# Experts' biases moved from the expert loop to the attention's projection, with gates in two parts

## What is computed

```python
xn = _layernorm(x, axis=-1)
x = x + _L0_attn_ref(xn, Wq, Wk, Wv, Wo) + _L0_ffn_ref(xn, Wg, bg, W1, b1, W2, b2)
# _L0_attn_ref: causal linear attention, Y @ Wo.T
# _L0_ffn_ref:
gate_probs = softmax(x @ Wg + bg)
_, top_idx = top_k(gate_probs, 2)
selected = gate_probs * expert_mask
selected = selected / (selected.sum(-1, keepdims=True) + 1e-08)
h = gelu(einsum('bsf,efh->bseh', x, W1) + b1)
expert_out = einsum('bseh,ehf->bsef', h, W2) + b2[None, None]
return einsum('bsef,bse->bsf', expert_out, selected)
# second layer: attention ends in  out = y @ w_proj + b_proj
```

## Time and profile before

| what | value |
|---|---|
| median of 3 runs | 354.57 us (354.26 to 354.77) |
| profiled execution | 354.33 us, its span 352.5 us |
| busy: PE, DVE, ACT, POOL | 339.4, 320.9, 271.4, 208.8 us |
| granted TensorE clock, mean | 0.995 |
| head and routing, to the first up product | 0 to 62.4 us |
| loop over slots | 62.4 to about 273 us |
| second layer | to 352.5 us |

### The profile page before, as it was taken

The page is one execution under the profiler, slowest core; times in us unless marked ns, Lnnn a source line. Parts: engine busy times, 40 slices in busy tenths (PEclk is TensorE's granted clock), DMA queues, the critical chain, the costliest instruction groups (busy, mean ns, idle before and its releaser), DMA issues.

```text
span 352.5 us, 9136 instructions
## 1 busy us (share of the span) xinstructions
PE 339.4 (96%) x2488; PEld 296.4 (84%) x2488; DVE 320.9 (91%) x633; ACT 271.4 (77%) x764; POOL 208.8 (59%) x229
## 2 busy tenths in 40 slices
PE   8999878999999999999999999999999899999995
PEld 3888334799999999999999899999998688778875
DVE  5999999899999999998899899998978799998665
ACT  2997946968887878787787678778985987777751
POOL 3899202843323666766776678778877278884110
PEclk9999989999999999999999999999999999999999
DMA  5896196454444555555555654565452002221112
GB/s 161 238 278 181 32 387 240 114 147 131 136 130 137 156 152 149 159 150 156 155 157 154 168 155 133 164 186 145 120 141 75 9 7 54 60 63 30 30 32 60
DMA packets 45520, 46.98 MB, mean 133 GB/s; under 512 B 6928, under 2 KB 33712, under 8 KB 45216
## 3 DMA queue, kind: packets, MB, share of 16 engines
q1 hardware_dynamic: 40432, 37.17, 35.7%
q0 software_dynamic: 4320, 8.86, 10.1%
q10 hardware_dynamic: 720, 0.38, 0.5%
HBM read 32.88 MB, written 13.50 MB: 132 GB/s over the span
## 4 chain that ended last, share of the span: by engine, by line
PE 86%; DVE 9%; DMA 2%; issue 2%; POOL 0%; ACT 0%; DVEq 0%; POOLq 0%
PE banks L574 18%; PE banks L561 18%; PE banks L700 7%; PE banks L701 7%; PE banks L364 4%; PE banks L1012 3%; PE banks L545 3%; PE banks L1041 2%; PE banks L1088 2%; PE banks L352 2%; PE banks L1070 2%; PE banks L1050 2%; PE banks L776 2%; PE banks L1022 2%; PE banks L1058 2%; PE banks L320 2%
## 5 line engine op out<-in xcount | busy, mean ns | idle before, releaser
L489 POOL DMA_INDIRECT xg<-xn_rows,slot_tok x71 | 76.5, 1077 | 77.0 <-PE banks L545 43.6
L591 ACT ACTIVATE xT<-banks,b1T 128x128 f32<-128x128 f32 x284 | 81.5, 375 | 18.8 <-PE banks L561 18.6
L506 POOL DMA_INDIRECT qk_exp<-expert_rows,ranki x64 | 74.0, 1156 | 19.1 <-issue 18.7
L574 PE MATMUL banks<-w_sb,xT 128*128 x568 | 78.9, 282 | 0.0
L561 PE MATMUL banks<-xgT,w 128*128 128x128 f32 x568 | 75.4, 276 | 0.0
L574 PEld LDWEIGHTS banks<-w_sb,xT 128*128 128x128 f32 x568 | 69.3, 192 | 0.5
L561 PEld LDWEIGHTS banks<-xgT,w 128*128 128x128 f32 x568 | 69.0, 192 | 0.8 <-issue 0.5
L712 DVE TENSOR_TENSOR cq<-banks,phi 128x360 f32<-128x360 f32 (+1 forms) x96 | 47.4, 548 | 7.6 <-PE banks L701 6.7
L684 DVE TENSOR_TENSOR low<-outer,high 128x1152 fp32r<-128x1152 f32 x32 | 43.5, 1358 | 3.2 <-ACT high L678 3.2
L721 DVE TENSOR_REDUCE sums<-cq 128x144 f32<-128x1152 f32 x32 | 43.0, 1343 | 0.1
L678 ACT CAST high<-outer 128x1152 fp32r<-128x1152 f32 x32 | 36.9, 1154 | 7.0 <-DVE outer L667 5.7
(11 more groups left out here) (210 smaller groups left out, 691.0 us busy)
## 6 DMA issues: line engine op xcount, KB each, us to landing
w<-in_L_ffn_W SPq DMA_DIRECT2D x71, 256.0 KB
expert_rows<-ye SPq DMA_DIRECT2D x71, 64.0 KB
expert_rows<-x_sb SPq DMA_DIRECT2D x2, 2048.0 KB, 9.7
x_sb<-in_L_attn_x SPq DMA_DIRECT2D x8, 256.0 KB, 4.0
xn_rows<-xn SPq DMA_DIRECT2D x8, 256.0 KB, 2.9
w_sb<-in_L_ffn_W SPq DMA_DIRECT2D x8, 256.0 KB, 3.9
out<-outer SPq DMA_DIRECT2D x7, 256.0 KB, 2.4
xg<-xn_rows,slot_tok POOLq DMA_INDIRECT x71
```

The source lines that it names most:

```text
L489: pool.indirect_dma_start(out=xg[n][:, :], out_offset=None, in_=xn_dram, in_offset=bass.IndirectOffsetOnAxis(ap=slot_tok[:, j:j + 1], axis ...
L506: pool.indirect_dma_start(out=y_moe[:, i, k, :], out_offset=None, in_=y_dram, in_offset=bass.IndirectOffsetOnAxis(ap=ranki[:, 0, k, i:i + ...
L574: last = nc.tensor.matmul(y, hidT[p][:, c, :], w2_sb[:, ds(e * NC + c, 1), :], start=False, stop=(c == NC - 1))
L591: last = nc.scalar.activation(hidT[p][:, c, :], slot_bank(j)[:, c * P:(c + 1) * P], ACT.Gelu_apprx_tanh, bias=b1T[:, ds(e * NC + c, 1)])
```

## The change

The bias matmul of each slot (L572) goes. b2 stands twice in a new tile `bias`: for the first tile of a batch in columns 0 to 127, for the second in columns 128 to 255, repeated on rows so that rows come in a high and a low part of b2 (`low_row`), each against a high and a low part of the gates. SP fills `bias_raw` by 16 DMAs of b2 (8 rows x 128) and two of b_proj (one row); they stand in its queue ahead of `save(0)`. ACT rounds the rows with low_row 1 (`bias_high`), POOL subtracts (`bias_parts`). DVE forms the gates of all experts (zero where not chosen) with three more operations, splits them in two parts (`split_gates`, two operations) between the first two `low`. PE transposes the split gates of two batches at a time, ACT copies them to `gT`, and one matmul per batch over 64 rows and 256 columns adds gates times bias at the projection. b_proj takes `ones_r` and `bias` in float32r in place of bf16.

```diff
+    bias_high_of = high[2][:, 0:NBIAS]
+    bias_raw = phi_all[:, 4 * D:4 * D + NBIAS]
+    gate_row = xn_all[:, 2:4, :, :].rearrange("p n c f -> p (n c f)")
+    gate_of_all = yT0[:, 0:NT * NE].rearrange("p (a e) -> p a e", e=NE)
...
-    def split_biases(pool):
...
+    def bias_high(act):
+        act.wait_ge(bias_loaded, 16 * 18)
+        nc.scalar.activation(bias_high_of, bias_raw, ACT.Copy, scale=const("low_row")).then_inc(bias_ready, 1)
+
+    def bias_parts(pool):
+        pool.wait_ge(bias_ready, 1)
+        nc.gpsimd.tensor_tensor(bias[:, :], bias_raw, bias_high_of.bitcast(f32), ALU.subtract).then_inc(bias_ready, 1)
...
-            pe.wait_ge(bias_rows, 16 * 6)
         y = slot_bank(j)[:, 0:D]
-        nc.tensor.matmul(y, ones_bf[:, :], bias3[:, ds(e * D, D)], start=True, stop=False)
...
+        if b == 0:
+            pe.wait_ge(gates_split, 1)
+        if b % 2 == 0:
+            nc.tensor.transpose(ps[6][:, 3 * P:4 * P], gate_row[:, b * NGR:(b + 2) * NGR], ident)
...
+        if b % 2 == 0:
+            nc.scalar.copy(gT[:, :], ps[6][:, 3 * P:4 * P])
...
+        rows = slice(b % 2 * NGR, (b % 2 + 1) * NGR)
+        nc.tensor.matmul(ps[5][:, 0:2 * D], gT[rows, :], bias[rows, 0:2 * D], start=False, stop=True,
+                         skip_group_check=True).then_inc(o_ps, 1)
...
-        nc.tensor.matmul(ps[4], ones_bf[:, :], bias3[:, BIASP:BIASP + D].unsqueeze(1).broadcast_to([P, GT, D]),
+        nc.tensor.matmul(ps[4], ones_r[:, :], bias[:, BIASP:NBIAS].unsqueeze(1).broadcast_to([P, GT, D]),
...
-            sp.dma_start(bias_sp[:, 0:BIASP // P], b2.rearrange("e h -> (e h)").rearrange("(p c) -> p c", p=P)).then_inc(bias_in, 16)
-            sp.dma_start(bias_sp[:, BIASP // P:NBIAS // P], b_proj.rearrange("(p c) -> p c", p=P)).then_inc(bias_in, 16)
...
+            sp.wait_ge(zeros_ready, 2)
+            for q in range(P // (2 * NE)):
+                for t in range(2):
+                    lo = (2 * q + t) * NE
+                    sp.dma_start(bias_raw[lo:lo + NE, t * D:(t + 1) * D], b2).then_inc(bias_loaded, 16)
+            for lo in (0, 32):
+                sp.dma_start(bias_raw[lo:lo + 1, BIASP:NBIAS], b_proj.rearrange("(a c) -> a c", a=1)
+                             ).then_inc(bias_loaded, 16)
...
-            sp.wait_ge(bias_split, 5)
-            sp.wait_ge(bias_zero, 1)
-            for n in range(3):
-                for lo, hi in ((0, BIASP), (BIASP, NBIAS)):
-                    sp.dma_start(bias3[n:n + 1, lo:hi].rearrange("a (p c) -> a p c", p=P),
-                                 bias_part[:, n, lo // P:hi // P]).then_inc(bias_rows, 16)
...
+            bias_high(act)
...
+                act.wait_ge(bias_ready, 2)
...
-            nc.vector.memset(bias3[:, :], 0.0).then_inc(bias_zero, 1)
+            nc.vector.memset(bias_raw, 0.0).then_inc(zeros_ready, 1)
...
+            both = TT(oh[:, 0, :, :], oh[:, 0, :, :], oh[:, 1, :, :], ALU.add)
...
-            done(RED(row(5), masked, AX.X, ALU.add))
+            RED(row(5), masked, AX.X, ALU.add)
+            v.wait_ge(route, n_route[0])
+            done(TT(gate_of_all, masked, oh[:, 0, :, :], ALU.mult))
...
+                done(TT(gate_of_all, gate_of_all, sel[0][:, :].unsqueeze(2).broadcast_to([P, NT, NE]), ALU.mult))
+
+            def split_gates():
+                whole = yT0[:, 0:NT * NE].rearrange("p (b f) -> p b f", b=B).unsqueeze(2).broadcast_to([P, B, 2, 2 * NE])
+                done(nc.vector.tensor_copy(gate_parts[:, :, :, 0, :], whole))
+                TT(gate_parts[:, :, :, 1, :], whole, gate_parts[:, :, :, 0, :].bitcast(f32), ALU.subtract
+                   ).then_inc(gates_split, 1)
...
             gates()
-            for r in range(2):
-                attn_low(v, 0, r, 0)
+            attn_low(v, 0, 0, 0)
+            split_gates()
+            attn_low(v, 0, 1, 0)
```

More of the change, by code:

```diff
@@ L22 @@
 BIG = 3.0e38
-BIASP, NBIAS = NE * D, NE * D + D
+BIASP, NBIAS = 2 * D, 3 * D
+NGR = 4 * 2 * NE
 CONSTS = {}
@@ L58, in constant_table @@
     put("row_no", row)
+    put("low_row", row // 32 % 2)
     put("rows_in_front", P * row)
@@ L99, in build @@
     NB = 4
-    xn = [sbuf(f"xn{p}", [P, GT, D]) for p in range(NB)]
+    xn_all = sbuf("xn_all", [P, NB, GT, D])
+    xn = [xn_all[:, p, :, :] for p in range(NB)]
     xT = [sbuf(f"xT{p}", [P, GT, P]) for p in range(2)]
@@ L118, in build @@
     bg_sb = sbuf("bg_sb", [P, NE])
[L119 to L122, removed]
+    bias = sbuf("bias", [P, NBIAS], f32r)
     ones_bf = sbuf("ones_bf", [P, P], bf16)
@@ L230, in build @@
     wT_ps, wT_ready = sem("wT_ps"), sem("wT_ready")
-    bias_in, bias_split, bias_rows = sem("bias_in"), sem("bias_split"), sem("bias_rows")
-    small_ready, pool_const, warmed, bias_zero = sem("small_ready"), sem("pool_const"), sem("warmed"), sem("bias_zero")
+    bias_in, bias_loaded, bias_ready = sem("bias_in"), sem("bias_loaded"), sem("bias_ready")
+    small_ready, pool_const, warmed, gates_split = sem("small_ready"), sem("pool_const"), sem("warmed"), sem("gates_split")
     zeros_ready = sem("zeros_ready")
@@ L569, in down @@
             pe.wait_ge(w2_in, 16 * NE)
-            pe.wait_ge(bias_rows, 16 * 6)
         y = slot_bank(j)[:, 0:D]
-        nc.tensor.matmul(y, ones_bf[:, :], bias3[:, ds(e * D, D)], start=True, stop=False)
         for c in range(NC):
             last = nc.tensor.matmul(y, hidT[p][:, c, :], w2_sb[:, ds(e * NC + c, 1), :],
-                                    start=False, stop=(c == NC - 1))
+                                    start=(c == 0), stop=(c == NC - 1))
         last.then_inc(down_ps, 1)
@@ L774, in attn_project @@
         pe.wait_ge(yT_ready, b + 1)
+        if b == 0:
+            pe.wait_ge(bias_ready, 2)
         for t in range(2):
-            last = nc.tensor.matmul(ps[5][:, t * D:(t + 1) * D], yT0[:, t * P:(t + 1) * P], wT[:, 0, :],
-                                    start=False, stop=True, skip_group_check=True)
-        last.then_inc(o_ps, 1)
+            nc.tensor.matmul(ps[5][:, t * D:(t + 1) * D], yT0[:, t * P:(t + 1) * P], wT[:, 0, :],
+                             start=False, stop=False, skip_group_check=True)
+        rows = slice(b % 2 * NGR, (b % 2 + 1) * NGR)
+        nc.tensor.matmul(ps[5][:, 0:2 * D], gT[rows, :], bias[rows, 0:2 * D], start=False, stop=True,
+                         skip_group_check=True).then_inc(o_ps, 1)
     def attn_x(act, b):
@@ L1138, in last_tensor @@
         for h in range(2):
-            nc.tensor.matmul(out_half(h), ones_bf[:, :], bias3[:, BIASP:BIASP + D].unsqueeze(1).broadcast_to([P, HALF, D]),
+            nc.tensor.matmul(out_half(h), ones_r[:, :], bias[:, BIASP:NBIAS].unsqueeze(1).broadcast_to([P, HALF, D]),
                              start=True, stop=False, skip_group_check=True)
@@ L1457, in _ @@
                     deviation(pool, 0, g + 5, g + 5)
-            split_biases(pool)
+            bias_parts(pool)
             pool.wait_ge(logits_read, 1)
@@ L1583, in choose @@
                 v.wait_ge(v_raw, NT // 2)
-                v.wait_ge(bias_in, 16 * 5)
+                v.wait_ge(bias_in, 16 * 3)
                 TT(lg, qkv3[:, :, 3 * D:NQ], per_expert(bg_sb[:, :]), ALU.add).then_inc(logits_read, 1)
@@ L1747, in _ @@
             for b in range(2):
+                if b == 1:
+                    v.wait_ge(bias_ready, 2)
                 phi(v, b, b)
```

19 lines of the change are left out of this document (6 added, 13 removed).

## The result

The changed kernel takes 362.29 us (median of 5 runs, 361.93 to 363.33), the kernel before 354.62 us beside it (5 runs). The ratio is 1.0207, with a 95% interval of 1.0178 to 1.0237: slower by 7.7 us. Forecast were 361.6 us, between 358.3 and 364.8. So the time is inside the range, and the first term is the head, as forecast. But several terms of the sum were off, one by a factor of four, and the total came out because they cancelled. What follows is about the terms.

The account below looks back on a forecast made before the run. PE was taken to set the loop's pace, DVE close behind. From 354.33 us, +8.0 for the head, +0.6 for DVE at the loop's start and -1.3 for PE in the loop gave 361.6 us, range 358.3 to 364.8.

Parts of the forecast that it names:

- the head: Before the routing: PE's stall, half-speed clock and a little catching up, 6.5 + 1.8 - 0.3 = +8.0 us.
- the loop: PE in the loop: bias matmuls removed, gate matmuls and transposes added, sum -1.3 us, between -2.0 and +4.9.
- stall of PE: Head, transposes of group 4: PE waits for ACT's normalising, held up by the late first save; +6.5 us.
- clock: Head, behind the stall: granted clock at half for 3.6 us of work, +1.8 us, bounds 0 and 3.6.
- catching up: Head, groups 4 to 5: time PE had lost to DVE comes back, -0.3 us.
- first `low`: Start of the loop: three new DVE operations delay the first `low` and PE's first sum; +0.6 us, between 0 and 1.9.
- The queue of SP: Head: eighteen small loads at 0.47 us each delay the save of group 0, whose landing ACT needs to reuse buffers.
- Rival 2: Head: no stall, if an issue takes under 0.11 us; 353.6 us in total, chance 0.09.
- Removed matmuls: Loop: 71 bias matmuls gone from PE at 0.058 us each, -4.1 us.
- Added matmuls: Loop: 16 float32r gate matmuls of 256 columns on PE at 0.12 us each, +1.95 us.
- Rival 4: Loop: the float32r matmul on 64 rows is as dear as float32, 0.51 us; 367.8 us in total, chance 0.05.
- Transposes: Loop: 8 added transposes of split gates on PE, +0.85 us.

Follow-up runs that it names:

- 128 rows alone: Changed kernel with the gate matmul over 128 rows instead of 64; 382.19 and 385.72 us on two slower chips, ratio to the kernel before 1.0045 and 1.0135.
- kept-busy kernel: Changed kernel plus 18 matmuls of zeros on PE during its stall; 383.95 and 388.02 us on two slower chips, ratio to the kernel before 1.0101 and 1.0129.
- loads alone: Kernel before plus sixteen loads of b2 to a spare buffer ahead of the first save; 360.24 us, ratio 1.0144.
- bias matmul moved: Kernel before with each slot's bias matmul behind the four down matmuls instead of ahead of them; 351.74 us, ratio 0.9908.
- both mended: Changed kernel with the small loads behind the saves of groups 4 to 6 and the gate matmul over 128 rows; 352.34 us, ratio 0.9936 to the kernel before.

## Why the prediction was right, and where its terms were wrong

The sign, the largest cause and its mechanism were right. That 361.6 came within 0.7 us of 362.29 was luck. The head was put 2.8 us too high (8.0 against 4.1 + 1.3 - 0.15) and the faster choosing of the experts left out (-0.8); the loop was put 3.3 us too low (-1.3 against +2.0). These errors cancel but for a few tenths. The lower end of the range, 358.3, isn't what its own terms give: 359.8 less the 0.7 us between -1.3 and -2.0 in the loop is 359.1. The measured time lies above both.

The ledger, by how much each point of the program lies later than before:

| Step | forecast | measured | how |
|---|---|---|---|
| this execution is late from its start | - | +0.4 | the step at 19.85 is at 19.45 before, and also with the same loads (128 rows alone) |
| stall of PE | +6.5 | +4.1 | transposes of group 4: 24.85 less 20.32, less 0.4 |
| clock | +1.8 | +1.3 | transposes to values: 2.61 less 1.30 |
| catching up | -0.3 | -0.15 | values of groups 4 to 7: 9.54 less 9.69 |
| choosing of the experts | 0 | -0.8 | first operation to scan: 6.69 less 7.50 |
| rest of the routing | 0 | -0.15 | first up product +4.72, scan +4.88 |
| first `low` | +0.6 | +0.6 | first sum +5.35, first up product +4.72 |
| loop | -1.3 | +2.0 | end of the loop (277.49 less 270.13) +7.36, first sum +5.35 |
| tail | 0 | +0.3 | spans: 360.2 less 352.5 |
| sum | +7.3 | +7.6 | |

**The queue of SP.** Mechanism, place and sign were right: issues first, then the landing of save(0), ACT, PE. The price of an issue was mis-sized. I took 0.47 us from the loads at this place, it was 0.36, a little under even the lower end (0.37, the loads of w1 in the earlier trace rows). Eighteen times that difference is 2 us of the 2.4 by which the forecast stall was too long; the rest is the 0.4 of the first row. Rival 2 needed 0.11 us; nothing came near. The Trainium skill, "DMA: Bandwidth & Descriptors", section "Anatomy of one DMA", gives about 50 ns for a sequencer's dispatch, on the path of gpsimd. Taken over to SP, that would have made the loads nearly free (an estimate: 18 x 0.05 = 0.9 us); SP took 0.36 us, seven times as long, so the figure doesn't carry over. The section "Issuing engines are not separate DMA queues" says that the issue is usually small relative to the DMA. The trace agrees (0.36 us against the 2.4 us of a save up to its landing), and it is no comfort here: the issue needn't be long against its own DMA, only queued ahead of somebody else's.

**The clock.** It fell to half for about 3 us, as forecast from the earlier trace rows. I priced 3.6 us at half speed at 1.8; it cost 1.3 to the values, of which the kept-busy kernel gives back 0.9 to 1.2. With the loads alone it stayed low for 6.0 us of work, and 2.7 us were lost from the transposes of group 4 to the choosing, so the 1.3 is what one execution shows and not the price of every such stall. The five executions of the changed kernel fit that: the mean granted clock is 0.991 in the two that take 361.93 and 362.01 us, and 0.985 or 0.986 in the three that take 362.29 to 363.33; that the difference lies in the head is not shown for these.

**DVE at the start of the loop.** +0.6 us as forecast. The split of the gates stayed hidden: the second group of sums comes 5.1 us later, less than the first.

**The loop.** Two terms failed, and this step had the wrong sign. Removed matmuls: 70 lie behind the first sum, 70 x 0.11 = -7.7 us; I took the distance from the bias matmul's start to the next, 0.058, and didn't ask what the group behind it would take without it. Added matmuls: 15 lie ahead of the loop's end, 15 x 0.51 = +7.7 us; I had scaled the running sums, which have the type but not the rows. Rival 4 had this number, 0.51 us, for another reason (that float32r would cost as float32) and at 0.05: its price came true, its reason didn't, since the same float32r matmul on 128 rows costs 0.13. Transposes: 8 x 0.11 = +0.9, as forecast. To these come 1.5 us of PE standing ahead of L550. Sum +2.4, measured +2.0. Both big terms were too small, by a factor of two and of four and with opposite signs, so they cancel each other but for 2.1 us; with the standing the loop is still 3.3 us off, and only the head's error hides that.

**The standing ahead of L550.** It grows as the down product gets shorter: 0.5 us before and with the loads alone (1.00 us for the down product), 1.2 with the bias matmul moved (0.95), 2.0 in the changed kernel and with both mended and 2.3 without the bias matmul (0.89). The profile names no releaser. L550 needs the rows that POOL gathers, and POOL works there without a pause (gathers and loads of `qk_exp` 0.3 us behind one another from 195 to 203 us). That the gather is what PE waits for is argued, not shown. I had asked only whether DVE would cap the gain, and it is POOL's side that took it, if anyone's.

**The choosing of the experts** wasn't in the sum at all, and gained 0.8 us; see the last section. The prediction had put `bias_parts` and POOL at nothing because POOL had time, and hadn't asked what POOL's work does to DVE beside it.

So of the 7.7 us the queue and the clock make 5.4, of which 0.95 come back by catching up and by the choosing. The 64-row matmul turned what would have been a gain of the loop of about 3 us (-7.7 + 15 x 0.13 + 0.9 + 1.5 = -3.3) into a loss of 2. The kernel with both mended has that gain: from the first running sum to the end of the loop it takes 198.1 us, against 201.9 before and 203.9 in the changed kernel.

## What to carry to other kernels

Small loads aren't small for the queue that issues them (0.34 to 0.36 us each here): before putting them in, look who saves or frees a buffer from the same queue behind them, and put them behind that. Price an instruction of TensorE by the distance over its whole neighbourhood, up to the second start behind it, with and without it; and where a matmul has fewer rows than its neighbours, try it padded with zeros (0.38 us a piece here). An equal type isn't an equal cost.

## What the runs showed of the hardware

**A matmul of 64 rows between such of 128** costs 0.51 us (256 columns, float32r), with zeros to 128 rows 0.13 us. The load itself takes as long (0.18 and 0.19 us); it is no longer ahead of its matmul, and neither is the load behind it. The Trainium skill, "TensorE: Matmul & The Clock Gate", section "Step-by-step: what each phase is for", says that weight loads are pulled ahead of running matmuls where the row groups don't conflict or the load goes to the background buffer, and that the number of rows doesn't matter to the time of a load. The second the trace agrees with; of the first it shows a case in which the pull ahead doesn't happen, and its price. Why it doesn't happen for 64 rows between 128 is not shown; only that the row number decides.

**VectorE beside GpSimd.** The operations of the choosing (DVE, then POOL), in the kernel before:

```profile
33.45 0.42 DVE L1592 TENSOR_REDUCE r<-outer 128x32 f32<-128x256 f32 x1
33.90 0.93 DVE L1593 TENSOR_TENSOR cq<-outer,r 128x256 f32<-128x256 f32 x1
34.87 1.38 DVE L1594 SCALAR_TENSOR_TENSOR outer<-cq,cst 128x256 f32<-128x256 f32 x1
...
29.34 6.62 POOL L422 TENSOR_TENSOR qkv<-qkv,qk_exp 128x512 f32<-128x512 f32 x5
```

and in the changed kernel:

```profile
39.59 0.42 DVE L1605 TENSOR_TENSOR cq<-outer,r 128x256 f32<-128x256 f32 x1
40.05 0.43 DVE L1606 SCALAR_TENSOR_TENSOR outer<-cq,cst 128x256 f32<-128x256 f32 x1
...
42.34 0.82 DVE L1605 TENSOR_TENSOR outer<-cq,r 128x256 f32<-128x256 f32 x1
...
41.87 1.01 POOL L414 TENSOR_TENSOR bias<-phi,high 128x384 fp32r<-128x384 f32 x1 [3.97 <-ACT high L410]
```

The same two operations (with two inputs in SBUF) take 0.93 and 1.38 us beside POOL's five, which end at 35.96, and 0.42 and 0.43 where POOL has nothing; the one beside the new `bias_parts` takes 0.82. The reduction, which has one input, takes 0.42 beside POOL too. In the changed kernel the stall let POOL finish first, hence the 0.8 us. The kernel with both mended has no stall and is as before, 7.80 us from first operation to scan against 7.50, since `bias_parts` now lies beside it as well. This fits the Trainium skill, "SBUF — State Buffer", section "Who interferes with whom": a VectorE instruction with two inputs in SBUF contends with a GpSimd instruction that reads SBUF. Not every such operation gets longer, though. The one ahead of them (L1585, at 32.99) takes 0.42 us beside POOL in the kernel before, and it is POOL's addition that takes 1.52 us there in place of 1.28; in the kernel with both mended the same operation takes 1.38. So an edit "at nothing" on POOL isn't at nothing if DVE is the path: I had looked only whether POOL had time.
